# Slot scatters of a fused clip, shared FFN and routing stage: issued in pairs behind product groups, from two sets of sources

## What is computed

```python
y = clip(einsum(x * styles, weight) * dcoefs + bias, -256, 256)       # a modulated 512x512 product
shared = (silu(y @ sh_gate_w) * (y @ sh_up_w)) @ sh_down_w            # HS = 1024
scores = sigmoid(y @ router_w.T); sb = scores + e_bias
# the best 4 of 8 groups of 8 experts, then the best 8 experts of the 32 left
topk_idx = top_k(where(emask, sb, -inf), 8)[1]
w = scores[topk_idx]; w = w / sum(w)
# every (token, expert) pair goes through its expert's FFN: 64 experts, H = 256
o = (silu(y[tok] @ gate_w[e]) * (y[tok] @ up_w[e])) @ down_w[e] * w
out = x + shared + zeros.at[tok].add(o)
```

## Time and profile before

| | |
|---|---|
| median of 3 runs | 4305.03 us (4304.62 to 4307.09) |
| the profiled execution | 4311.05 us, of which the span of its instructions is 4309.3 us |
| TensorE busy | 3985.9 us (92%), 19154 matmuls |
| TensorE weight loads | 3223.3 us (75%) |
| VectorE busy | 1653.4 us (38%) |
| ScalarE busy | 1434.4 us (33%) |
| GpSimd busy | 1941.6 us (45%), of it the 512 slot scatters 511.1 us |
| granted TensorE clock, mean | 0.963 |

### The profile page before, as it was taken

The page is one execution under the profiler, slowest core; times in us unless marked ns, Lnnn a source line. Parts: engine busy times, 40 slices in busy tenths (PEclk is TensorE's granted clock), DMA queues, the critical chain, the costliest instruction groups (busy, mean ns, idle before and its releaser), DMA issues.

```text
span 4309.3 us, 90207 instructions
## 1 busy us (share of the span) xinstructions
PE 3985.9 (92%) x19154; PEld 3223.3 (75%) x19155; DVE 1653.4 (38%) x3502; ACT 1434.4 (33%) x2806; POOL 1941.6 (45%) x1598
## 2 busy tenths in 40 slices
PE   7888888888988885999999999999799999999997
PEld 6777767777777764888878887787578888888886
DVE  4444444444544552333333333333533333333332
ACT  3222222222222212343343344343533443443333
POOL 1233333322322343555555555555455555555554
PEclk9999989999999997999999999999999999999999
DMA  4111111111111103666676666666866666666665
GB/s 164 40 40 42 42 40 54 40 49 49 40 39 40 39 30 80 112 123 111 110 137 110 112 123 131 124 120 123 227 129 115 124 120 113 123 126 122 112 112 103
DMA packets 372955, 408.67 MB, mean 95 GB/s; under 512 B 192457, under 2 KB 227409, under 8 KB 372881
## 3 DMA queue, kind: packets, MB, share of 16 engines
q0 software_dynamic: 135872, 280.60, 36.3%
q1 hardware_dynamic: 237010, 127.35, 11.0%
HBM read 228.83 MB, written 178.93 MB: 95 GB/s over the span
## 4 chain that ended last, share of the span: by engine, by line
PE 43%; DMA 8%; SPq 5%; issue 4%; DVE 1%; DVEq 0%; ACT 0%; POOLq 0%; ACTq 0%; POOL 0%
PE bank L1087 26%; PE bank L1105 12%; DMA out_dram<-o_rows,list_s 4%; PE bank L1078 3%; SPq L934 3%; PE bank L1096 2%; DMA raw_d<-in_L_ffn_down_w_dram 2%; DMA list_g<-slot_list 1%; SPq L969 1%; DMA raw_gu<-in_L_ffn_up_w_dram 1%; SPq L986 0%; DVE w_dn_l L30 0%; DMA list_s<-slot_list 0%; ACT o_rows L1168 0%; POOLq L934 0%
## 5 line engine op out<-in xcount | busy, mean ns | idle before, releaser
L1040 POOL DMA_INDIRECT out_dram<-o_rows,list_s x532 | 864.8, 1625 | 772.8 <-DMA list_g<-slot_list 408.7
L400 POOL DMA_INDIRECT slot_list<-ent,pos x512 | 511.1, 998 | 1074.7 <-DVE ent L768 917.1
L1087 PE MATMUL bank<-w_gu_h,x_h 128*128 x2128 | 886.8, 417 | 42.5 <-DVE w_dn_l L30 42.2
L1087 PE MATMUL bank<-w_gu_h,x_l 128*128 x2128 | 844.9, 397 | 0.0
L1087 PE MATMUL bank<-w_gu_l,x_h 128*128 x2128 | 834.3, 392 | 0.0
L1024 POOL DMA_INDIRECT x_rows<-y_rows,list_g x536 | 546.6, 1020 | 484.6 <-issue 294.0
L1244 DVE TENSOR_TENSOR e_hf<-bank,e_sg 128x256 f32<-128x256 f32 x532 | 226.0, 425 | 1080.7 <-ACT e_sg L1154 577.2
L30 DVE TENSOR_TENSOR x_l<-bank,x_h 128x512 fp32r<-128x512 f32 x533 | 368.4, 691 | 653.0 <-ACT x_h L1148 427.2
L1148 ACT CAST x_h<-bank 128x512 fp32r<-128x512 f32 x533 | 313.4, 588 | 633.2 <-PE bank L1078 589.8
L1087 PEld LDWEIGHTS bank<-w_gu_h,x_h 128*128 128x128 f32 x2128 | 401.3, 189 | 113.1 <-issue 46.7
L1154 ACT ACTIVATE e_sg<-bank 128x256 f32<-128x256 f32 x532 | 204.9, 385 | 842.2 <-PE bank L1087 761.2
(11 more groups left out here) (203 smaller groups left out, 5803.8 us busy)
## 6 DMA issues: line engine op xcount, KB each, us to landing
xin<-in_x_dram SPq DMA_DIRECT2D x16, 1024.0 KB
y_rows<-yrow SPq DMA_DIRECT2D x64, 256.0 KB
stage_d<-in_x_dram SPq DMA_DIRECT2D x16, 1024.0 KB, 5.3
out_dram<-stage_d SPq DMA_DIRECT2D x16, 1024.0 KB, 4.6
raw_gu<-in_L_ffn_gate_w_dram SPq DMA_DIRECT2D x29, 512.0 KB
raw_gu<-in_L_ffn_up_w_dram SPq DMA_DIRECT2D x29, 512.0 KB
raw_d<-in_L_ffn_down_w_dram SPq DMA_DIRECT2D x29, 512.0 KB
list_g<-slot_list SPq DMA_DIRECT2D x536, 1.0 KB
```

Source lines behind the costliest of these rows:

```text
L400: nc.gpsimd.indirect_dma_start(slots, bass.IndirectOffsetOnAxis(ap=pos[:, t, k:k + 1], axis=0), ent[:, t, k, :], None).then_inc(scattered, 16)
L1040: nc.gpsimd.indirect_dma_start(out, bass.IndirectOffsetOnAxis(ap=ls[u][:, 0:1].bitcast(U32), axis=0), og[u][:], None, compute_op=ALU.add). ...
L1087: last = nc.tensor.matmul(b_gu[u % 2][:], xp[a][:, u % 2, k, :], wgu[b][:, bass.ds(place, 1), k, :].rearrange("p a n -> p (a n)"), start=( ...
```

## The change

The sources of the scatters, `pos` and `ent`, exist twice, and so does the semaphore `scattered`; even blocks use set 0, odd blocks set 1. VectorE's wait before it overwrites a set is now for the scatters of the block two before. Before each even `k` GpSimd waits for a further product group of TensorE: the pair number (8t + k)/2 of block `i`, counted from 0, waits for the gate and the up group in turn, from the gate of chunk 5 of block `i` on, one group a pair. The sixteenth pair so waits for the up group of chunk 4 of block `i + 1`. The last block's scatters don't wait in this way. Number, size and order of the scatters, and their places in `slot_list`, stay. The loops of GpSimd and VectorE are peeled to match: on VectorE four blocks stand outside the loop instead of two, on GpSimd the loop takes two blocks a turn.

```diff
--- before.py
+++ after.py
@@ -310,8 +310,8 @@
             i8 = sb("i8", [P, TT, TOPK], U32)
             i8f = sb("i8f", [P, TT, TOPK])
             pf = sb("pf", [P, TT, TOPK])
-            pos = sb("pos", [P, TT, TOPK], U32)
-            ent = sb("ent", [P, TT, TOPK, 2], I32)
+            pos = [sb(f"pos{n}", [P, TT, TOPK], U32) for n in range(2)]
+            ent = [sb(f"ent{n}", [P, TT, TOPK, 2], I32) for n in range(2)]
             den = sb("den", [P, TT])
             rden = sb("rden", [P, TT])
 
@@ -330,7 +330,8 @@
             pe_g, act_sg, pe_u, dve_h = sem("pe_g"), sem("act_sg"), sem("pe_u"), sem("dve_h")
             act_hh, dve_hl, pe_d, dve_o = sem("act_hh"), sem("dve_hl"), sem("pe_d"), sem("dve_o")
             dve_cur, dve_mask, pe_rank, dve_rank = sem("dve_cur"), sem("dve_mask"), sem("pe_rank"), sem("dve_rank")
-            dve_ent, scattered = sem("dve_ent"), sem("scattered")
+            dve_ent = sem("dve_ent")
+            scattered = [sem("scattered0"), sem("scattered1")]
             tab_ok, tab_st, table_chain = sem("tab_ok"), sem("tab_st"), sem("table_chain")
             pool_split = sem("pool_split")
             steps = sem("route_steps")
@@ -392,23 +393,32 @@
 
             @blk.gpsimd
             def _(pool):
-                def body(i):
+                def body(i, v, paced):
+
                     for t in range(TT):
                         pool.wait_ge(dve_ent, TT * i + t + 1)
                         pool.nop(nofuse=True)
                         for k in range(TOPK):
+                            if paced and k % 2 == 0:
+                                chunk = NCH * i + NCH - 2 + (TOPK * t + k) // 4
+                                pool.wait_ge(pe_g if k % 4 == 0 else pe_u, chunk)
+                                pool.nop(nofuse=True)
                             nc.gpsimd.indirect_dma_start(
-                                slots, bass.IndirectOffsetOnAxis(ap=pos[:, t, k:k + 1], axis=0),
-                                ent[:, t, k, :], None).then_inc(scattered, 16)
+                                slots, bass.IndirectOffsetOnAxis(ap=pos[v][:, t, k:k + 1], axis=0),
+                                ent[v][:, t, k, :], None).then_inc(scattered[v], 16)
 
 
                 nc.gpsimd.tensor_copy(sdw[0][:], stage_d[:]).then_inc(pool_split, 1)
                 pool.wait_ge(pool_split, 1)
                 nc.gpsimd.tensor_tensor(sdw[1][:], stage_d[:], sdw[0][:].bitcast(F32), ALU.subtract).then_inc(pool_split, 1)
                 pool.wait_ge(filled, 48)
-                with pool.Fori(0, NBLK) as i:
-                    body(i)
-                pool.wait_ge(scattered, 16 * TOPK * TT * NBLK)
+                body(0, 0, True)
+                with pool.Fori(0, NBLK // 2 - 1) as g:
+                    body(2 * g + 1, 1, True)
+                    body(2 * g + 2, 0, True)
+                body(NBLK - 1, 1, False)
+                for v in range(2):
+                    pool.wait_ge(scattered[v], 16 * TOPK * TT * NBLK // 2)
 
             @blk.tensor
             def _(pe):
@@ -690,7 +700,7 @@
                 def by_group(ap):
                     return ap.rearrange("p t (g e) -> p t g e", g=GROUPS)
 
-                def routing(i):
+                def routing(i, g, v):
 
                     n = [0]
 
@@ -751,9 +761,9 @@
                     ranked = misc[0][:, 0:TT * E].rearrange("p (t e) -> p t e", t=TT)
                     link(nc.vector.tensor_tensor(sl[:], ranked, base[:].unsqueeze(1).to_broadcast([P, TT, E]), ALU.add))
                     nc.vector.tensor_tensor(base[:], misc[0][:, TT * E:(TT + 1) * E], base[:], ALU.add).then_inc(dve_rank, 1)
-                    if some(16 * TOPK * TT * i):
-                        dve.wait_ge(scattered, 16 * TOPK * TT * i)
-                    link(nc.vector.tensor_copy(ent[:, :, :, 0], tok[:].unsqueeze(2).to_broadcast([P, TT, TOPK])))
+                    if some(g):
+                        dve.wait_ge(scattered[v], 16 * TOPK * TT * g)
+                    link(nc.vector.tensor_copy(ent[v][:, :, :, 0], tok[:].unsqueeze(2).to_broadcast([P, TT, TOPK])))
                     link(nc.vector.tensor_scalar(tok[:], tok[:], float(TB), None, ALU.add))
                     yield
                     for t in range(TT):
@@ -762,10 +772,10 @@
                                                      i8f[:, t, :].unsqueeze(2).to_broadcast([P, TOPK, E]), ALU.is_equal))
                         link(nc.vector.tensor_tensor(oh2[:], oh[:], sl[:, t, :].unsqueeze(1).to_broadcast([P, TOPK, E]), ALU.mult))
                         link(nc.vector.tensor_reduce(pf[:, t, :], oh2[:], AX_X, ALU.add))
-                        nc.vector.tensor_copy(pos[:, t, :], pf[:, t, :])
+                        nc.vector.tensor_copy(pos[v][:, t, :], pf[:, t, :])
                         link(nc.vector.tensor_tensor(oh2[:], oh[:], wn[:, t, :].unsqueeze(1).to_broadcast([P, TOPK, E]), ALU.mult))
                         link(nc.vector.tensor_reduce(v8[:, t, :], oh2[:], AX_X, ALU.add))
-                        nc.vector.tensor_scalar(ent[:, t, :, 1].bitcast(F32), v8[:, t, :], rden[:, t:t + 1], None,
+                        nc.vector.tensor_scalar(ent[v][:, t, :, 1].bitcast(F32), v8[:, t, :], rden[:, t:t + 1], None,
                                                 ALU.mult).then_inc(dve_ent, 1)
                         yield
                     assert n[0] == STEPS, n[0]
@@ -774,8 +784,8 @@
                 pieces_of = {0: 1, 1: 1, 2: 1, 3: 1, 4: 2, 5: 1, 6: 2}
                 pieces_of_last = {0: 2, 1: 1, 3: 3, 4: 3}
 
-                def body(i, prep, v):
-                    pieces = routing(i)
+                def body(i, g, prep, v):
+                    pieces = routing(i, g, v)
                     for c in range(NCH):
                         hidden(i, c)
                         if prep and c == 0:
@@ -877,11 +887,13 @@
                     y_clip(0, m)
                 y_low(0, 0)
                 logits(0)
-                body(0, True, 0)
-                with dve.Fori(0, NBLK // 2 - 1) as g:
-                    body(2 * g + 1, True, 1)
-                    body(2 * g + 2, True, 0)
-                body(NBLK - 1, False, 1)
+                body(0, 0, True, 0)
+                body(1, 0, True, 1)
+                with dve.Fori(1, NBLK // 2 - 1) as g:
+                    body(2 * g, g, True, 0)
+                    body(2 * g + 1, g, True, 1)
+                body(NBLK - 2, NBLK // 2 - 1, True, 0)
+                body(NBLK - 1, NBLK // 2 - 1, False, 1)
         dense.close()
 
 
```

## The result

The changed kernel takes 4074.56 us in the median of 4 runs (4070.02 to 4089.86), the kernel before 4305.63 us beside it (4304.62 to 4307.09). The ratio is 0.9469, 95% interval 0.9444 to 0.9495. The profiled execution of the changed kernel took 4089.86 us (span 4088.2 us) and is the slowest of the four.

The account below looks back on a forecast made before the run. TensorE was taken to bound the dense stage, stopped by holes during GpSimd's scatter bursts. Profiled 4311.05 - 237.9 (holes) + 3 (last block) = 4076.2, less 6.0 to the median gives 4070 us, range 4050 to 4150.

Parts of the forecast that it names:

- The holes: Dense stage: TensorE stalls during GpSimd's scatter bursts, 15.86 us a block, 237.9 us over 15 blocks, all expected to go.
- The clean chunk of 9.16 us: Chunk 5 spared a hole while scatters ran beside it; taken twice, for chunks 5 and 6, in the hole-free block.
- The clean period: Dense-stage block without a hole, pieced together as 64.96 + 18.32 = 83.28 us, against 99.14 us measured before.
- +3: End of the dense stage: the last block's scatters were expected to end later, adding 3 us to the sum.
- 6.0 us: Whole kernel: difference between profiled execution and median before the change, taken off 4076.2 us to give 4070 us.
- The store that fills: Dense stage: an unnamed store that scatters fill, full after 18.5 us, some 15 scatters in a row doing no harm.
- emptying rate: Dense stage: the store was estimated to empty at 0.59 per us or more, above the paced 0.38 and 0.51.
- The rule of the DMA page: DMA engines alternate between queues packet by packet, so spreading tiny packets gains nothing: 4308 us; the rows were preferred.
- The last block: Its 32 scatters stay a burst and its hole stays; last scatter at most 4.1 us later, +3 taken.
- No effect by code position: Rival: TensorE's hole belongs to its code at chunks 5 and 6, as if awaiting instructions; 4308 us, chance 0.07.
- Part of the holes stays: Rival: the store empties more slowly or counts pairs, leaving 2 to 8 us a block; 4100 to 4190 us, chance 0.07.
- A second hole at the store of `out`: Rival: scatters beside a bulk store stop TensorE, adding a hole in chunk 0 of each block; 4546 us, chance 0.05.

Follow-up runs that it names:

- e1: Changed kernel without the waits for product groups (second set of sources, second semaphore and peeled loops kept): ratio 1.0018 to the kernel before, block period 101.3 us.
- e9: Kernel before, one set of sources, a small memset and a wait for it behind every scatter, no wait for TensorE: ratio 0.9486, 4094.8 us.
- e12: The changed kernel itself, measured again beside the kernel before on the same chip: ratio 0.9459, 4083.27 us, block period 83.3 us.
- e2: Changed kernel paced by tile, only the first scatter of each tile waiting, so four bursts of 8: ratio 0.9411, 4086.6 us.
- e3: Changed kernel paced by two tiles, so two bursts of 16 scatters a block: ratio 0.9912, 4303.1 us, block period 98.0 us.
- e4: Kernel before with one set of sources, its 32 scatters spread two or three behind each of 12 product groups: ratio 0.944, 4099.3 us.
- e7: Kernel before, unpaced, each scatter turned into a plain DMA of the same 128 entries; only dense stage compared: block period 83.2 us.
- e5: Kernel before, unpaced, every scatter cut to the first 64 of its 128 rows; only dense stage compared: block period 100.8 us.
- e6: Kernel before, unpaced, each scatter turned into a gather of the same 128 rows; only dense stage compared: block period 99.6 us.
- e8: Changed kernel with its scatters in bursts of 12, 12 and 8 a block: ratio 0.9609, 4146.6 us, block period 88.2 us.

## Why the prediction was right

The forecast was 4070 us, the median is 4074.56. Point by point:

- **The holes are what the change removes, and they go in full.** In the profile after no "issue" gap on TensorE lies beside a scatter from block 0 to 14. e1 shows that the waits do it, not what came with them, and e9 that a distance of 2 us between the scatters does it without a wait for TensorE. The clean chunk of 9.16 us, taken from the one block where chunk 5 had been spared, stood in all fifteen.
- **The size.** The clean period was put at 83.28 us; e12 has 83.3, the profiled execution 83.95. The difference in the latter, 10 us in all, is the three pauses at the loop's end, which the rows of the kernel before don't show and the sum has no term for. The trace of e12 has none of them.
- **The sum against the profiled execution.** Spans: 15 x (99.14 - 83.95) = 227.9 us less; end of the dense stage 4.3 us later (from block 15's first product with up to the expert stage's first transpose 112.7 against 108.4; +3 was predicted); setup 4.5 us longer, which the change doesn't touch and the sum left out; expert stage 2.1 us shorter. 227.9 - 4.3 - 4.5 + 2.1 = 221.2, and the spans are 221.1 apart. Forecast for the profiled execution were 4076.2 us, and it took 4089.86; the expert stage was to begin near 1435 us and begins at 1449.9. That the medians agree to 4.6 us is partly luck: the forecast took off 6.0 us from the profiled execution to the median, as in the kernel before, and in the changed kernel they are 15.3 us apart.
- **The store that fills.** The picture was useful, its limit was off. It was read as 15 scatters in a row that do no harm. e2 has the first late message after seven, e3 the first gap of TensorE at the 12th, and in the kernel before itself the word of the gate group done by 625.78 took 17 us, while the earlier trace rows, which the limit was read from, show TensorE alone, still full then. With that limit two bursts of 16 were expected to cost 8 us a block; they cost 14.7 (e3). Its emptying rate was bounded at 0.59 per us or more. e9 at 0.47 and e4 at 0.58 over 55 us are without a hole, which agrees but doesn't test it: no run lies between these and the full 0.77. For pairs, at 0.38, neither mattered.
- **The rule of the DMA page.** The Trainium skill, DMA: Bandwidth & Descriptors, Queues, rings and completion order, has each DMA engine take turns between its queues packet by packet; the forecast that the change brings nothing (4308 us) was my reading of that. e7 agrees, with 128-entry DMAs at 0.53 us each and no hole; the hole of the scatters isn't that kind of thing, since it stays with half the rows (e5) and with reads in place of writes (e6).
- **The last block.** The burst's last scatter was put at 4.1 us later at most, with steps of 1.27 us; the steps of the earlier trace rows are 1.33 in the mean (41.36 us for 31), which gives 5.6. Measured from the same product of block 15 it goes 2.5 us later.
- **The rivals.** No effect by code position: refuted, the position of the code is the same and the hole is gone; the row that the prediction took for a `turn_x` is one of the last matmuls of an up group, with the `turn_x` right behind it, and another place of the program all the same; e3 has holes at chunk 1, where the kernel before never had one. Part of the holes stays: not with pairs; it is what e8 shows. A second hole at the store of `out`: none in the profile after.

What stays open is the resource. Shown is that indirect DMAs on GpSimd, 1.27 us apart, delay first what TensorE tells others and then its own instructions, with 128 rows or 64 and in either direction; and that plain DMAs of the same size don't. Whether TensorE's updates, the records of its instructions or both are what can't get out wasn't told apart: every run here was recorded, so a run without recording might differ, in the hole and in the gain. The traces give a hint that it is worth asking. Each scatter makes 16 completion updates, 8192 in the dense stage, and the traces hold 2617 of them in the kernel before, 2354 in e3, 3137 in e2, 5380 in the changed kernel, 7454 in e9 and all 8192 in e7, where the DMAs are plain and come 0.53 us apart. So records are lost where the indirect DMAs come fast, and the mere number of updates isn't what loses them. The Trainium skill, NOTIFIC — the notification-queue block, The write path, says that the block which writes such records can hold back its producers when it is full; no run here shows whether that is what happened.

## What to carry to other kernels

A wait put down to "issue" on one engine, at a place where it should wait for nothing, is to be laid beside what the other engines do at that time, above all beside a block in which one of them paused by itself. Indirect DMAs from GpSimd are better spread over a stage than issued as the data come: here a burst of 8 cost next to nothing, one of 12 2.5 us, one of 16 7.4 and one of 24 15.9, and 32 of them 2 us apart nothing. A wait on GpSimd for progress of the engine that is the bound spreads them, and so does a filler behind each (e9), if the end of the stage doesn't wait for the last one; a second set of sources is needed only if the last scatter would otherwise come after the next write.

## What the runs showed of the hardware that wasn't expected

- Indirect DMAs of 128 rows of 8 bytes, 1.27 us apart on GpSimd, make TensorE's semaphore updates arrive late, by some 3 us after seven of them (e2) and by 17 us after ten in a burst of 24 (kernel before), and hold its instructions to one in 0.7 to 2 us after 12 to 15. With 64 rows (e5) and as gathers (e6) the hole is the same. 2.07 us apart they don't (e9).
- A plain DMA of the same 128 entries takes 0.53 us of GpSimd, a scatter 0.96 and 0.30 to the next.
- Behind the idle 2.17 us at the loop's end TensorE went on at the lower of its two clocks (1.2 GHz; the granted clock is 0.61 over 657.2 to 660.5), with steps of 0.43 us for 512 columns, and came back to the full one (2.4 GHz) with steps of 0.23.
- The traces hold a third of the completion updates of scatters 1.27 us apart (2617 of 8192), nine tenths of them 2.07 us apart (7454) and all of those of plain DMAs 0.53 us apart (e7).
